# Three buffers of edge lists in a graph layer: lists and dst rows asked for three double tiles ahead

## The chip, the cores and the metric

The kernel runs on one core of one Trainium2 chip. The metric is the device time of one execution in microseconds (us). The core's engines are TensorE (PE), VectorE (DVE), ScalarE (ACT), GpSimd (POOL) and SyncE (SP, which here only asks for DMAs). A profile page and a trace of one execution go with it.

## The reference

```python
h = jnp.maximum(_layernorm(x, axis=-1), 0.0)          # x: 6250 nodes x 64
msg = h[src] + edge_attr_64                            # 206250 edges, sorted by dst
agg = jax.ops.segment_sum(msg, dst, num_segments=6250)
x = x + (jax.nn.relu(agg @ W1 + b1) @ W2 + b2)         # W1: 64x128, W2: 128x64
```

Each node sums the normalized rows of its source nodes and the features of its edges, and a small two-layer network is applied to the sum.

## The kernel before

The 6250 nodes are 49 tiles of 128. They are worked in double tiles of 256 nodes: DTS = 25 of them, numbered 0 to LAST = 24, where the last holds one tile that is cut in halves of HALF = 56.

Sum over source nodes: for a double tile the kernel makes a matrix of counts (how often does source node s feed node i) and multiplies it with h. Steps for double tile j:

- `gather_rows(j)` (POOL, indirect DMA): for each node the row of 66 sorted dst values in which its first edge lies, into g2.
- `count_below(j)` and `set_pointers(j)` (DVE): compare and reduce g2, giving the number of the node's first edge: ell_idx and rp_f.
- `place_ranges(j)` (POOL, two small instructions): first edge of each tile, r0_i. SP reads it and loads with it dst rows (`load_dst_rows`) and edge features (`load_edges`, four slots).
- `gather_slots(j)` (POOL, two indirect DMAs of 128 rows): the 64 list entries from each node's first edge on, out of comb_dram (the combined list that the kernel writes first), into ell. This is the edge list.
- `match(j)` (DVE): marks entries of other nodes, hi_m. `turn_codes(j)` (PE) transposes, `take_codes(j)` (ACT) copies to codes.
- `hots(j, b)` (DVE): one-hots lo_hot and hi_hot of five batches b (25 or 26 pairs of nodes); `count(j, u)` (PE) multiplies them, and ACT copies the counts.
- `high_sums`, `low_sums` (PE): counts times h, one double tile later, interleaved with the counts of the next.

Sum over edge features: `make_rel(j)` (POOL) turns dst rows to positions, `turn_rel(j)` (PE) transposes them, `take_rel(j)` (ACT) copies, `edge_hots(j, h)` (DVE) makes one-hots, `edge_sums` (PE) multiplies with the edges.

Every engine runs its own list of instructions in order. In DVE's loop step j the batches of `hots(j, .)` come with, in between, `edge_hots(j - 1, .)`, `match(j + 1)`, `add_rows(j - 2)`, and `count_below(j + 2)` and `set_pointers(j + 2)` behind batches 1 and 2. In PE's loop step j come the five rounds of `count(j, .)` with the sums of j - 1, the last layers of j - 2, and, in round 2, `turn_codes(j + 1)` and `turn_rel(j)`. POOL's loop is the one in the printed code below. `rest_of_h` and `rest_of_rest`, two long DVE instructions, lie behind batches 0 and 2 of double tile 0. Semaphores order the engines: a gather waits until its buffer is read (`turned`, `below_made`) and its index is made (`idx_made`); SP waits for `r0_made`, `rel_made` and `edges_done` and, at the end of its step, for `rows_added` in store_rows.

The second half-tile of the last double tile needs pointers moved by 72 partitions: PE does this with a matmul into shift_ps, and DVE copies it to ell_idx (`shifted`, `shift_made`), in loop step LAST - 2.

## Time and profile before

| what | value |
|---|---|
| median of 3 runs | 521.38 us (519.58 to 523.01) |
| the profiled execution | 519.95 us |
| its span in the trace | 518.2 us |
| mean granted clock of TensorE | 0.992 |
| PE busy | 459.3 us, 89% |
| DVE busy | 435.2 us, 84% |
| ACT busy | 380.2 us, 73% |
| POOL busy | 322.5 us, 62% |

The span is the time from the first to the last instruction that the trace shows; the execution's own time has a little more around it. Busy time counts an engine's instructions without its waits. An indirect DMA counts as busy on POOL for as long as POOL works or is held in it. PEld is PE's loading of weights, which runs beside its matmuls.

### The profile page before, as it was taken

How to read it: one execution, taken by the hardware profiler on the slowest of the kernel's cores; microseconds unless marked ns; L12 is line 12 of the kernel's file. 1: busy time of each engine (PE TensorE's matmuls, PEld its weight loads, DVE VectorE, ACT ScalarE, POOL GpSimd, SP SyncE). 2: the span in 40 equal slices, each digit the busy share in tenths (PEclk: the TensorE clock that was granted, in tenths of full speed). 3: DMA queues.
4: the chain of work that ended last, by engine and by line, in shares of the span. 5: the costliest groups of instructions: out<-in, count | busy, mean ns of one | idle time of the engine just before them, and what ended most of it. 6: DMA issues, size and time to landing. Idle time of an engine off the chain costs nothing.

```text
span 518.2 us, 27591 instructions
## 1 busy us (share of the span) xinstructions
PE 459.3 (89%) x12541; PEld 405.9 (78%) x12541; DVE 435.2 (84%) x531; ACT 380.2 (73%) x481; POOL 322.5 (62%) x223
## 2 busy tenths in 40 slices
PE   1012799999999999999999999999999999999994
PEld 1002688898889888888888988988898898888883
DVE  4989977988988998998898899889889988969550
ACT  2846766787878787787878878878787887878720
POOL 4379998976676566657756666756757675125200
PEclk9999989999999999999999999999999999999997
DMA  9758057643663474466357346536744643661200
GB/s 203 186 142 259 19 145 198 203 133 111 185 187 103 141 200 121 114 187 171 97 159 201 107 126 193 150 94 178 195 108 130 198 131 99 185 182 51 78 3 10
DMA packets 139626, 73.65 MB, mean 142 GB/s; under 512 B 23644, under 2 KB 137550, under 8 KB 139382
## 3 DMA queue, kind: packets, MB, share of 16 engines
q1 hardware_dynamic: 136105, 65.30, 45.8%
q0 software_dynamic: 3168, 4.90, 3.5%
q8 instruction: 100, 1.64, 1.2%
q10 hardware_dynamic: 234, 1.65, 1.0%
q14 instruction: 19, 0.16, 0.1%
HBM read 66.98 MB, written 4.86 MB: 139 GB/s over the span
## 4 chain that ended last, share of the span: by engine, by line
PE 84%; POOL 6%; DMA 3%; ACT 2%; DVE 2%; issue 1%; SPq 0%; ACTq 0%; DVEq 0%; POOLq 0%
PE sum_ps L844 25%; PE sum_ps L866 21%; PE count_ps L831 17%; PE sum_ps L852 14%; POOL ell L509 3%; PE sum_ps L881 3%; PE sum_ps L888 3%; POOL g L489 2%; DMA comb_rows<-counts 1%; PE sum_ps L816 1%; DMA dst_sb<-in_dst 1%; DMA ell<-comb_rows,ell_idx 1%; ACT counts L343 1%; ACT counts L345 1%; POOL r_f L496 1%
## 5 line engine op out<-in xcount | busy, mean ns | idle before, releaser
L407 ACT CAST counts<-count_ps 128x882 bf16<-128x882 f32 (+2 forms) x369 | 327.0, 978 | 60.2 <-PE count_ps L831 59.1
L675 DVE TENSOR_TENSOR lo_hot<-iota_lo,codes 128x3328 bf16<-128x3328 bf16 (+3 forms) x123 | 229.9, 1869 | 41.3 <-PE count_ps L831 25.0
L509 POOL DMA_INDIRECT ell<-comb_rows,ell_idx x50 | 105.2, 2103 | 90.2 <-DVE ell_idx L647 56.5
L844 PE MATMUL sum_ps<-counts,h_parts 128*128 128x256 bf16 (+1 forms) x1225 | 145.4, 273 | 0.0
L844 PEld LDWEIGHTS sum_ps<-counts,h_parts 128*128 128x128 bf16 x1225 | 114.5, 99 | 18.2
L831 PE MATMUL count_ps<-hi_hot,lo_hot 64*128 64x49 bf16 x6256 | 110.4, 183 | 16.8 <-DVE hi_hot L675 14.8
L831 PEld LDWEIGHTS count_ps<-hi_hot,lo_hot 64*128 64x128 bf16 x6256 | 96.0, 94 | 37.3 <-DVE hi_hot L675 19.6
L489 POOL DMA_INDIRECT g<-in_dst,row_i x49 | 95.5, 1949 | 37.9 <-DVE e_hot L689 21.3
L866 PE MATMUL sum_ps<-e_hot,edges 128*64 128x24 f32 x3528 | 112.9, 217 | 1.0 <-issue 1.0
L866 PEld LDWEIGHTS sum_ps<-e_hot,edges 128*64 128x64 f32 x3528 | 107.7, 138 | 3.7 <-issue 1.1
L675 DVE TENSOR_TENSOR hi_hot<-iota_hi,codes 128x1300 bf16<-128x1300 bf16 (+3 forms) x123 | 103.9, 844 | 0.0
L852 PE MATMUL sum_ps<-counts,h_parts 128*64 128x256 bf16 (+1 forms) x1225 | 81.1, 273 | 0.3 <-issue 0.3
L852 PEld LDWEIGHTS sum_ps<-counts,h_parts 128*64 128x64 bf16 x1225 | 62.0, 111 | 6.1 <-issue 5.7
L520 POOL TENSOR_SCALAR rel_rows<-dst_rows,tile_base 36x256 f32<-36x256 int32 (+1 forms) x25 | 47.7, 1910 | 24.3 <-DMA dst_rows<-in_dst 23.4
L689 DVE TENSOR_TENSOR e_hot<-win_tab,rel_sb 128x864 f32<-128x864 f32 x49 | 53.0, 1081 | 5.7 <-ACT rel_sb L381 5.7
L390 ACT COPY agg_sb<-sum_ps 128x256 f32<-128x256 f32 (+1 forms) x25 | 9.2, 367 | 36.3 <-PE sum_ps L852 36.3
L528 POOL TENSOR_TENSOR x_sb<-x_sb,b_all 128x128 f32<-128x128 f32 (+1 forms) x25 | 28.2, 1130 | 1.6
L805 PE MATMUL sum_ps<-ident_b,ell 128*128 128x128 bf16 x25 | 5.6, 224 | 21.7 <-DVE hi_m L661 21.7
L499 POOL CAST r_i<-r_f 1x2 int32<-1x2 f32 x24 | 22.9, 954 | 1.5
L805 PEld LDWEIGHTS sum_ps<-ident_b,ell 128*128 128x128 bf16 x25 | 2.8, 113 | 22.2 <-issue 19.3
L496 POOL TENSOR_SCALAR r_f<-rp_f 1x2 f32<-1x2 f32 x24 | 17.3, 722 | 2.5 <-DVE rp_f L649 1.9
L372 ACT COPY codes<-sum_ps 128x512 bf16<-128x512 bf16 x25 | 14.8, 593 | 5.4 <-PE sum_ps L806 5.4
(107 smaller groups left out, 213.7 us busy)
## 6 DMA issues: line engine op xcount, KB each, us to landing
edges<-in_edge_attr SPq DMA_DIRECT2D x98, 576.0 KB, 5.2
h_rows<-h_sb SPq DMA_DIRECT2D x1, 1568.0 KB, 10.3
x_sb<-in_x SPq DMA_DIRECT2D x4, 384.0 KB, 10.2
out<-o_sb SPq DMA_DIRECT2D x24, 64.0 KB, 1.7
comb_rows<-counts ACTq DMA_DIRECT2D x1, 1443.8 KB
dst_rows<-in_dst SPq DMA_DIRECT2D x49, 18.0 KB
ell<-comb_rows,ell_idx POOLq DMA_INDIRECT x50
g<-in_dst,row_i POOLq DMA_INDIRECT x49, 4.0
```

The costliest lines, as they stand in the source:

```text
L407: nc.scalar.copy(counts[j % 2][:, :, 0:2 * half].rearrange("p s (h i) -> p h s i", h=2)[:, :, :, first + a:first + b], count_ps[u % 3][:, ...
L489: nc.gpsimd.indirect_dma_start(out=g2[j % 2][:, h, :], out_offset=None, in_=dst.rearrange("(r e) -> r e", e=STEP), in_offset=bass.Indirect ...
L499: nc.gpsimd.tensor_copy(r0_i[0:1, 2 * j:2 * j + n], r0_f[0:1, 2 * j:2 * j + n]).then_inc(r0_made, 1)
L509: nc.gpsimd.indirect_dma_start(out=ell[j % 2][0:rows, h, :, :].rearrange("p s w -> p (s w)"), out_offset=None, in_=comb_dram[:, :], in_off ...
L520: nc.gpsimd.tensor_scalar(rel_rows[j % 2][0:n * CK, :], dst_rows[j % 2][0:n * CK, :], float(2 * j * P), tile_base[0:n * CK, 0:1], ALU.subt ...
L528: nc.gpsimd.tensor_tensor(x_sb[:, tiles, :], x_sb[:, tiles, :], bc(b2_all[:, :].rearrange("p (o f) -> p o f", o=1), [P, tiles_in(f), F]), ...
L675: return nc.vector.tensor_tensor(out_ap.rearrange("p i (a t) -> p i a t", t=2), bc(table_ap.rearrange("p (o a t) -> p o a t", o=1, t=2), [ ...
L689: nc.vector.tensor_tensor(e_hot[h][:, :, :].rearrange("p (c k) w -> p c k w", k=KK), bc(win_tab[:, m // LAST, :, :].rearrange("p c (o w) - ...
L831: last = nc.tensor.matmul(count_ps[u % 3][:, h, i * NT:(i + 1) * NT], lo_hot[n % 2][rows, a + i, :], hi_hot[n % 2][rows, a + i, 0:NT], sta ...
L844: nc.tensor.matmul(sum_ps[m % 2][:, 0:cols], parts[:, s, 0:2 * F], counts[m % 2][:, s, 0:cols], start=(s == 0), stop=False, skip_group_che ...
L852: last = nc.tensor.matmul(sum_ps[m % 2][half, 0:cols], parts[:, s, 2 * F:3 * F], counts[m % 2][:, s, 0:cols], start=False, stop=False, ski ...
L866: last = nc.tensor.matmul(sum_ps[m % 2][half, low:low + W], edges[t % SLOT_EDGES][:, c, k * F:(k + 1) * F], e_hot[h][:, i, :], start=False ...
```

## The change

The number of ell buffers goes from two to AHEAD = 3, with a semaphore each. POOL issues gather_rows 0 to 3, gather_slots 0 to 2, place_ranges 0 to 2 and make_rel(0) before its loop, which starts with double tile 3; in the loop make_rel and add_bias are one step further behind. DVE does `count_below(2)` before `match(0)`, `set_pointers(2)` after it, and in its loop counts and points for j + 3. The shift for the last double tile moves to loop step LAST - 3. g2, ell_idx, dst_rows, rel_rows and codes keep two buffers. The diff, without lines that only replace `j % 2` by `j % AHEAD` for ell:

```diff
+    AHEAD = 3
-        ell = [sb(f"ell{b}", [P, 2, SLOTS, 2], i32) for b in range(2)]
+        ell = [sb(f"ell{b}", [P, 2, SLOTS, 2], i32) for b in range(AHEAD)]
-        shift_ps = sum_ps[LAST % 2][:, 260:261]
+        shift_ps = sum_ps[(LAST - AHEAD) % 2][:, 260:261]
-        ell_in = [sem("ell_in0"), sem("ell_in1")]
+        ell_in = [sem(f"ell_in{b}") for b in range(AHEAD)]
...
-                    if j >= 2:
-                        pool.wait_ge(turned, j - 1)
+                    if j >= AHEAD:
+                        pool.wait_ge(turned, j - AHEAD + 1)
...
                 gather_rows(0)
-                for j in range(DTS):
-                    if j >= 3:
-                        pool.wait_ge(e_hots, 2 * (j - 3) + 1)
+                gather_rows(1)
+                place_ranges(0)
+                gather_rows(2)
+                pool.wait_ge(comb_out, 48)
+                gather_slots(0)
+                gather_slots(1)
+                place_ranges(1)
+                make_rel(0)
+                gather_rows(3)
+                gather_slots(2)
+                place_ranges(2)
+                for j in range(AHEAD, DTS):
+                    if j >= 4:
+                        pool.wait_ge(e_hots, 2 * (j - 4) + 1)
                     if j + 1 < DTS:
                         gather_rows(j + 1)
-                    if j == 0:
+                    gather_slots(j)
+                    if j < LAST:
                         place_ranges(j)
-                        pool.wait_ge(comb_out, 48)
-                    gather_slots(j)
-                    if 1 <= j < LAST:
-                        place_ranges(j)
-                    if j >= 1:
-                        make_rel(j - 1)
-                    if j >= 2:
-                        add_bias(j - 2)
+                    make_rel(j - 2)
+                    add_bias(j - 3)
+                make_rel(DTS - 2)
+                add_bias(DTS - 3)
+                make_rel(DTS - 1)
                 add_bias(DTS - 2)
                 add_bias(DTS - 1)
-                make_rel(DTS - 1)
...
                 normalize()
+                count_below(2)
                 match(0)
+                set_pointers(2)
...
-                        if b == 4 and j == LAST - 2:
+                        if b == 4 and j == LAST - AHEAD:
...
-                        if b == (1 if j + 2 < LAST else 0) and j + 2 < DTS:
-                            count_below(j + 2)
-                        if b == (2 if j + 2 < LAST else 1) and j + 2 < DTS:
-                            set_pointers(j + 2)
+                        if b == (1 if j + AHEAD < LAST else 0) and j + AHEAD < DTS:
+                            count_below(j + AHEAD)
+                        if b == (2 if j + AHEAD < LAST else 1) and j + AHEAD < DTS:
+                            set_pointers(j + AHEAD)
...
-                                if m == LAST - 2:
+                                if m == LAST - AHEAD:
                                     pe.wait_ge(shift_made, 1)
...
-                        if j == LAST - 2 and v == 3:
+                        if j == LAST - AHEAD and v == 3:
                             pe.wait_ge(rp_made, DTS)
-                            pe.wait_ge(codes_made, LAST)
-                            pe.wait_ge(rel_copied, LAST - 1)
+                            pe.wait_ge(codes_made, LAST - AHEAD + 2)
+                            pe.wait_ge(rel_copied, LAST - AHEAD + 1)
```

## Rows read from the trace of the kernel before

**Rows 1.** Stretches by double tile: length, busy us of each engine, clock, DMA.
```profile
33.80:57.06 23.26, 7.21 (x262) 6.08 (x262) 23.23 (x21) 18.06 (x18) 22.09 (x8) 1.00 0.73 215
57.06:79.35 22.29, 21.23 (x502) 17.98 (x503) 19.29 (x22) 14.94 (x19) 20.96 (x9) 0.92 0.40 113
79.35:98.77 19.42, 18.37 (x511) 16.29 (x510) 16.12 (x20) 14.63 (x19) 17.49 (x9) 1.00 0.67 169
...
118.84:137.09 18.25, 18.25 (x515) 16.23 (x509) 16.37 (x20) 14.66 (x20) 12.95 (x9) 1.00 0.52 149
```

**Rows 2.** Timeline of DVE: start, us, line, output and inputs, idle before it.
```profile
32.07 0.48 DVE L661 SCALAR_TENSOR_TENSOR hi_m<-ell,node_f 128x64 bf16<-128x64 f32 x2
33.79 1.89 DVE L675 TENSOR_TENSOR lo_hot<-iota_lo,codes 128x3328 bf16<-128x3328 bf16 x1 [1.25 <-ACT codes L372]
...
42.23 0.57 DVE L626 TENSOR_TENSOR below<-g,node_f 128x132 bf16<-128x132 int32 x1
...
45.58 3.42 DVE L641 TENSOR_TENSOR h_parts<-counts 128x3136 bf16<-128x3136 f32 x1
...
49.31 0.15 DVE L647 TENSOR_TENSOR ell_idx<-cnt,row_base 128x2 int32<-128x2 f32 x1
...
61.72 0.29 DVE L633 TENSOR_REDUCE cnt<-below 128x2 f32<-128x132 bf16 x1
...
67.38 0.48 DVE L661 SCALAR_TENSOR_TENSOR hi_m<-ell,node_f 128x64 bf16<-128x64 f32 x2 [2.82 <-DMA ell<-comb_rows,ell_idx]
```

**Rows 3.** Timeline of POOL from 27 to 66 us.
```profile
27.01 1.00 POOL L509 DMA_INDIRECT ell<-comb_rows,ell_idx  x1 [4.85 <-DMA comb_rows<-counts]
...
29.56 1.61 POOL L489 DMA_INDIRECT g<-in_dst,row_i  x1 [0.30 <-issue]
31.47 1.50 POOL L489 DMA_INDIRECT g<-in_dst,row_i  x1 [0.30 <-issue]
...
34.52 1.98 POOL L509 DMA_INDIRECT ell<-comb_rows,ell_idx  x1 [0.30 <-issue]
36.52 3.31 POOL L496 TENSOR_SCALAR r_f<-rp_f 1x2 f32<-1x2 f32 x1
...
46.13 3.70 POOL L489 DMA_INDIRECT g<-in_dst,row_i  x1 [0.30 <-issue]
50.13 12.38 POOL L509 DMA_INDIRECT ell<-comb_rows,ell_idx  x1 [0.30 <-issue]
62.81 1.81 POOL L509 DMA_INDIRECT ell<-comb_rows,ell_idx  x1 [0.30 <-issue]
...
65.20 1.15 POOL L520 TENSOR_SCALAR rel_rows<-dst_rows,tile_base 36x256 f32<-36x256 int32 x1
```

**Rows 4.** Timeline of PE: head, and one of the middle.
```profile
58.57 4.18 PE L844 MATMUL sum_ps<-counts,h_parts 128*128 128x256 bf16 x20
...
69.16 0.43 PE L816 MATMUL sum_ps<-wide,rel_rows 36*128 36x36 f32 x2
70.52 0.81 PE L831 MATMUL count_ps<-hi_hot,lo_hot 64*128 64x49 bf16 x50 [0.93 <-DVE hi_hot L675]
...
119.38 2.35 PE L844 MATMUL sum_ps<-counts,h_parts 128*128 128x256 bf16 x20
```

**Rows 5.** Stretches of one us: PE busy, granted clock, DMA share, GB/s.
```profile
72.00:73.00 1.00, 1.00 (x36) 0.79 0.37 108
...
75.00:76.00 1.00, 1.00 (x33) 0.50 0.49 99
```

**Rows 6.** All gathers of g: from the DMA to its landing, us.
```profile
DMA to landing us min/median/max: 2.3/4.0/6.9
```

**Rows 7.** Timeline of SP's queue: dst rows of double tile 1 asked.
```profile
42.45 0.82 SPq L284 DMA_DIRECT2D dst_rows<-in_dst  x2
```

**Rows 8.** Timeline of DVE: the shifted pointer of the last double tile.
```profile
462.20 0.15 DVE L774 CAST ell_idx<-sum_ps 56x1 int32<-56x1 f32 x1 [3.87 <-PE sum_ps L938]
```

**Rows 9.** Timeline of POOL in the middle: first gather of a list.
```profile
415.56 2.38 POOL L509 DMA_INDIRECT ell<-comb_rows,ell_idx  x1 [2.98 <-DVE ell_idx L647]
```

More of the change, by code:

```diff
@@ L509, in gather_slots @@
                         nc.gpsimd.indirect_dma_start(
-                            out=ell[j % 2][0:rows, h, :, :].rearrange("p s w -> p (s w)"), out_offset=None,
+                            out=ell[j % AHEAD][0:rows, h, :, :].rearrange("p s w -> p (s w)"), out_offset=None,
                             in_=comb_dram[:, :],
                             in_offset=bass.IndirectOffsetOnAxis(ap=ell_idx[j % 2][0:rows, h:h + 1], axis=0)
-                        ).then_inc(ell_in[j % 2], 16)
+                        ).then_inc(ell_in[j % AHEAD], 16)
                 def make_rel(j):
@@ L652, in match @@
                 def match(j):
-                    dve.wait_ge(ell_in[j % 2], 32 * (j // 2 + 1))
+                    dve.wait_ge(ell_in[j % AHEAD], 32 * (j // AHEAD + 1))
                     if j >= 2:
                         dve.wait_ge(turned, j - 1)
-                    words = ell[j % 2][:, :, :, :].rearrange("p h s w -> p (h s w)")
+                    words = ell[j % AHEAD][:, :, :, :].rearrange("p h s w -> p (h s w)")
                     nodes, his = words.bitcast(f32)[:, 1::2], words.bitcast(bf16)[:, 1::4]
@@ L803, in turn_codes @@
                         pe.wait_ge(rows_added, j - 2)
-                    los = ell[j % 2][:, :, :, :].rearrange("p h s w -> p (h s w)").bitcast(bf16)[:, 0::4]
+                    los = ell[j % AHEAD][:, :, :, :].rearrange("p h s w -> p (h s w)").bitcast(bf16)[:, 0::4]
                     nc.tensor.transpose(codes_ps(j)[:, 0:P], los, ident_b[:, :])
```

## The prediction, on record before the change was run

> **What bounds the kernel now.** I read the busy shares first, then the busy time by double tile, then the timelines of TensorE (PE), VectorE (DVE) and GpSimd (POOL) over the first 120 us, then what happens around the last double tiles. PE is busy 89% of the 518.2 us (the table above). By stretch: the one from 118.84 to 137.09 is a plain double tile of the middle, 18.25 us long with PE busy 18.25 us [rows 1]. Nothing that lets POOL or DVE run earlier can shorten such a stretch. Where PE is not full is the head: 7.2 of 23.3 us while double tile 0 is counted (33.80 to 57.06), 21.2 of 22.3 us in the next one, 18.4 of 19.4 us in the one after [rows 1]. The change can win or lose only there, and perhaps at the tail, where the shifted pointer is made.
>
> In the stretch of double tile 0 DVE is busy 23.2 of 23.3 us [rows 1]: it makes the one-hots and both rests of h, and PE waits for it. So whatever is added to DVE there, or makes it wait, delays the end one for one. In the stretch of double tile 1 the one wait that matters is `match(2)`: DVE idles 2.82 us until the list of double tile 2 lands [rows 2]. That list is late because of POOL: its first gather takes 12.38 us, beside DVE's one-hots, against 1.00 us for the first of list 0 [rows 3]. PE is then idle 0.93 us before the counts of batch 3 [rows 4], and from 72 to 76 us the granted clock falls to 0.79 and then 0.50, the lower of TensorE's two levels (1.2 of 2.4 GHz), and is 1.00 again after it; what PE did before was to stand idle those 0.93 us [rows 4, 5].
>
> **What can be won.** 0.93 us of idle time, and the clock. Four microseconds at 0.79, 0.50, 0.50 and 0.50 (the two outer rows are shown, the two between read 0.50) are 4 - 2.29 = 1.7 us of full-speed work lost [rows 5]. Together 2.6 us, if the match no longer waits, if the clock then holds, and if nothing else is late. The 20 matmuls that took 4.18 us at 58.57 against 2.35 us in the middle [rows 4] lost 1.8 us more at the start of PE's dense work; the change gives PE no earlier work, so I leave that term as it is. The 1.05 us that PE lacks in the stretch from 79.35 is a gap inside a run of matmuls with no wait in the code between them, so it stays.
>
> **What the change adds ahead of the one-hots.** `count_below(2)` now runs before `match(0)`. Its rows are gathered at about 22.3 us, while POOL in the kernel before stood idle 4.85 us for the combined list to be written [rows 3], so they are there. It is one compare and one reduce. In the loop the compare took 0.57 us beside a POOL instruction and the reduce 0.29 [rows 2]; without POOL each takes about 0.3, so 0.6 us. DVE has no gap before `match(0)` at 32.07 [rows 2], and everything after hangs on it: +0.6 us. (If the list of double tile 0 landed just at 32.07, a part of it would be hidden: 0 to 0.6.) `set_pointers(2)`, 0.15 us, lies in the 1.25 us that DVE waits for the codes [rows 2]: 0.
>
> **What POOL does in the new order.** After gather_slots(0) (ended 29.26 in the old order) come, in place of gather_rows(2), the gathers of list 1 with the same durations beside the same normalization, 1.61 and 1.50 us [rows 3], so to 33.0; place_ranges(1), two instructions of 0.2 us as DVE is mostly idle, to 33.4; make_rel(0), 1.15 us [rows 3], to 34.6. In the old order place_ranges(1) came beside DVE's work: its r_f alone was held from 36.52 to 39.83 [rows 3], and make_rel(0) came behind. So POOL is some 9 us earlier. Its next work is gather_rows(3), from 34.8 us, beside the one-hots. Each gather here ends 0.85 us after the end of some DVE instruction: 34.52 + 1.98 = 36.50, where lo_hot ended at 35.68; 46.13 + 3.70 = 49.83, where the second rest ended at 49.00 [rows 2, 3]. With DVE 0.6 us later the first half ends at 37.1 and the second, started behind the rest of h, 3.7 us after 37.4: 41.1.
>
> **The new wait.** DVE wants those rows early: the old `count_below(2)` at 42.23 [rows 2] found rows gathered at 29.56 to 32.97. The new `count_below(3)` stands in the same place, 42.8, and its gather ended only at 41.1. From the end of a gather to its landing it takes 2.3, 4.0 or 6.9 us (min, median, max) [rows 6]. Landing at 45.1 by the median, DVE waits 2.3 us, with 0.6 and 5.2 as the bounds. I take the median, as the edge loads of double tiles 0 and 1 are in flight: four are asked right behind match(0), and the next four come some 5 us earlier than they did, since dst rows 1 no longer wait for place_ranges(1) until 42.45 [rows 7]. Behind the waiting instruction on DVE are the one-hots of batches 2 to 4, and PE waits for those. This is in the stretch bound by DVE, so all of it counts.
>
> **The sum.** +0.6 + 2.3 - 0.9 - 1.7 = +0.3 us. While DVE waits, POOL has free room, so gather_slots(2) ends near 45 and list 2 lands before 50, against `match(2)` at 67.38 now [rows 2]: that wait is gone for certain.
>
> **The loop.** In loop step j POOL now does gather_rows(j+1), gather_slots(j), place_ranges(j), make_rel(j-2), add_bias(j-3), with its first wait one double tile earlier; DVE counts and points three ahead. The distance of each make_rel from its use on PE is unchanged, and the same number of instructions run in each double tile: 0 against a PE that is full. SP's queue, which asks for dst rows, is still held by `edges_done` (four edge slots) and by store_rows, and dst_rows has two buffers still, so past double tile 2 these come no earlier. Three list buffers give only slack. At the tail the shifted pointer moves from double tile LAST-2 to LAST-3 with the same waits; DVE idled 3.87 us for it before 462.20 [rows 8], while PE was busy all of that stretch. POOL's make_rel(22) is now queued behind it: a plain double tile earlier is 444, two gathers and it make 448, and PE turns rel 22 in the round before 462, near 458. I count 0. `count_below(5)` in the stretch from 79.35 may wait for its rows, but DVE has 3.3 us of reserve there (busy 16.1 of 19.4) [rows 1].
>
> **Rival 1, slower: make_rel(1) comes late.** On POOL make_rel(1) stands behind gather_slots(3), which must wait for set_pointers(3), at the place of the old set_pointers(2), 49.31 [rows 2]. The old order had the same queue: gather 12.38 us, until the compare before the reduce at 61.72 was over [rows 2, 3], gather 1.81, then make_rel(1) at 65.20 for PE's use at 69.16 [rows 3, 4]. But there DVE then stood still for 2.82 us, and POOL's small instructions ran free. Without that pause they meet the match and one-hots: r_f and r_i then take 0.4 to 5 us (3.31 for r_f beside the rest of h [rows 3]) and make_rel(1) up to 3, so it ends between 66.5 and 72, on DVE's own time, and PE, which wants it at 69.0, waits up to 3 us with all its counts behind, and DVE and ScalarE (codes of double tile 2 stand behind rel) after it. If the second gather is held as long as the first was, it is freed only when DVE runs dry: 64.56 and 0.6 for match and pointers and two batches of 2.5 us (67.38 + 0.6 to 70.5, when PE starts [rows 2, 4]) make 70.1, then 0.85, place_ranges and make_rel until 72.6: 3.5 us. It decides from the point where POOL is over 2.5 us later than before. Against it: in the middle the same gather after the same pointers can take 2.38 us [rows 9], not 12.38. Its time: +0.6 + 2.3 + 3 - 0.9 = +5.0, the clock loss staying: 526.4.
>
> What the rows show is that a gather beside DVE sometimes gets in at the next end of a DVE instruction (2.38 [rows 9], 1.98) and sometimes passes over ten of them (12.38) [rows 3]. The Trainium skill, SBUF — State Buffer, section "SBUF: two separate sides", says that VectorE and GpSimd share a port pair by an exclusive lock held for one whole instruction, the loser waiting until it ends; by that the gather of 12.38 us would have ended near 52 us, and make_rel(1) would always be in time, which takes Rival 1 away and leaves the forecast. The trace disagrees with its 12.38 us, so Rival 1 keeps its chance.
>
> **Rival 2, a small gain.** The rows of double tile 3 land in time: the landing takes 2.3 us, or the gather gets in at a free moment, and the 0.6 us is partly hidden. Then +0.3 + 0.3 - 2.6 = -2.0: 519.4. For it: half of the landings are under 4.0 us. Against: the edge loads.
>
> **Rival 3, nothing at all at either place.** The new wait is there but the clock dips anyway, since PE's idle time while double tile 0 is counted grows: +0.6 + 2.3 - 0.9 = +2.0: 523.4.
>
> **How the numbers follow.** The profiled execution took 519.95 us, 1.75 more than its span and 1.4 less than the median of the three runs, 521.38; I add the sum to the median: 521.7. Chances: forecast 0.35, Rival 1 0.22, Rival 2 0.23, Rival 3 0.20. All but the far end of Rival 1 is within 1% (5.2 us, about what a measurement here can tell from nothing). For the range I take Rival 2 less the spread of the runs shown (1.8): 517.6, and Rival 1 at the top: 526.5. Faster by over 1% needs 516.2 or less, over twice what the head offers: 0.02. Slower by over 1% needs a stall of PE over 3.2 us on top of the late rows: 0.10. Else 0.88.
>
> **What the changed profile would show.** Right: the middle still 18.25 us with PE full; DVE idle before the compare of `count_below(3)` near 43 us, released by the DMA of g; no idle before hi_m near 67; list gathers 0 and 1 done by 33 us; the first batch of double tile 1 on PE near 60 us instead of 57.06; the granted clock at 1.00 through 72 to 80. Wrong: if that DVE wait is missing, Rival 2; if PE idles before the transposes of rel_rows (L816 of before) near 72 us, Rival 1; a middle stretch of other than 18.2 us would upset the whole reading.

## The result, and the profile after

The changed kernel takes 526.89 us (median of 4 runs, 523.18 to 529.62) beside 521.57 of the kernel before (4 runs, 519.58 to 523.01): a ratio of 1.0103, 95% interval 1.0068 to 1.0138. It is slower by about 1%. The profiled execution took 525.78 us, with a span of 524.0 us and a mean granted clock of 0.982 (before: 519.95, 518.2 and 0.992).

The stretches by double tile of the changed kernel, cut at the same events as [rows 1] (columns: stretch and length, busy us of PE, PEld, DVE, ACT and POOL, granted clock, DMA share, GB/s):

```profile
34.40:60.28 25.88, 7.21 (x260) 6.08 (x262) 23.06 (x21) 18.09 (x18) 18.47 (x10) 1.00 0.66 197
60.28:85.11 24.83, 22.25 (x504) 19.16 (x504) 19.30 (x21) 14.86 (x19) 23.00 (x15) 0.86 0.35 100
85.11:107.33 22.22, 21.45 (x512) 18.40 (x510) 16.71 (x21) 14.65 (x19) 11.92 (x9) 0.85 0.74 191
107.33:125.58 18.25, 18.25 (x510) 16.23 (x509) 16.10 (x20) 14.72 (x19) 12.20 (x9) 1.00 0.51 148
```

The plain double tile is 18.25 us with PE full, as in [rows 1]: three buffers cost nothing in such a stretch. The three stretches ahead of it grew by 2.6, 2.5 and 2.8 us. In the first, DVE's busy time is unchanged (23.06 for 23.23) in a longer stretch, so DVE waits. In the next two the clock column fell to 0.86 and 0.85, from 0.92 and 1.00.

DVE's timeline of the changed kernel, against [rows 2]:

```profile
32.71 0.47 DVE L670 SCALAR_TENSOR_TENSOR hi_m<-ell,node_f 128x64 bf16<-128x64 f32 x2
...
45.71 0.29 DVE L635 TENSOR_TENSOR below<-g,node_f 128x132 bf16<-128x132 int32 x1 [2.75 <-DMA g<-in_dst,row_i]
...
52.55 0.15 DVE L656 TENSOR_TENSOR ell_idx<-cnt,row_base 128x2 int32<-128x2 f32 x1
...
64.63 0.28 DVE L635 TENSOR_TENSOR below<-g,node_f 128x132 bf16<-128x132 int32 x1
64.94 0.29 DVE L642 TENSOR_REDUCE cnt<-below 128x2 f32<-128x132 bf16 x1
...
67.70 0.48 DVE L670 SCALAR_TENSOR_TENSOR hi_m<-ell,node_f 128x64 bf16<-128x64 f32 x2
...
72.42 0.81 DVE L684 TENSOR_TENSOR hi_hot<-iota_hi,codes 128x1250 bf16<-128x1250 bf16 x1
```

`match(0)` starts 0.64 us later, `count_below(3)` waits 2.75 us for its rows, and `match(2)` at 67.70 waits for nothing where it waited 2.82 us. Now POOL in the same time, against [rows 3]:

```profile
34.91 2.31 POOL L490 DMA_INDIRECT g<-in_dst,row_i  x1 [0.17 <-issue]
37.53 3.71 POOL L490 DMA_INDIRECT g<-in_dst,row_i  x1 [0.30 <-issue]
41.54 1.49 POOL L510 DMA_INDIRECT ell<-comb_rows,ell_idx  x1 [0.30 <-issue]
43.33 0.95 POOL L510 DMA_INDIRECT ell<-comb_rows,ell_idx  x1 [0.30 <-issue]
...
52.96 12.78 POOL L510 DMA_INDIRECT ell<-comb_rows,ell_idx  x1 [5.78 <-DVE ell_idx L656]
66.05 1.82 POOL L510 DMA_INDIRECT ell<-comb_rows,ell_idx  x1 [0.30 <-issue]
67.89 0.20 POOL L497 TENSOR_SCALAR r_f<-rp_f 1x2 f32<-1x2 f32 x1
68.16 5.10 POOL L500 CAST r_i<-r_f 1x2 int32<-1x2 f32 x1
73.36 1.16 POOL L521 TENSOR_SCALAR rel_rows<-dst_rows,tile_base 36x256 f32<-36x256 int32 x1
```

List 2 is gathered at 41.54 and 43.33, 8.6 us ahead of the old 50.13 of [rows 3]. The lead that POOL had won stops at 52.96: `gather_slots(3)` needs pointers that DVE makes at 52.55, so POOL stood idle 5.78 us. The gather then takes 12.78 us and ends at 65.74, 0.83 us after the compare that runs until 64.91. The cast of two numbers behind it is held 5.10 us, until the last one-hot is done at 73.23 and DVE has run dry. `make_rel(1)` ends at 74.52. PE had wanted it 2.45 us earlier (against [rows 4]):

```profile
60.28 1.58 PE L842 MATMUL count_ps<-hi_hot,lo_hot 64*128 64x49 bf16 x52 [0.66 <-DVE hi_hot L684]
61.79 3.85 PE L855 MATMUL sum_ps<-counts,h_parts 128*128 128x256 bf16 x20
...
74.58 0.31 PE L827 MATMUL sum_ps<-wide,rel_rows 36*128 36x36 f32 x1 [2.45 <-POOL rel_rows L521]
...
85.87 0.70 PE L892 MATMUL sum_ps<-agg_sb,w_sb 128*128 128x256 f32 x2
...
92.05 2.04 PE L877 MATMUL sum_ps<-e_hot,edges 128*64 128x24 f32 x36 [0.77 <-issue]
```

And the stretches of one us of the changed kernel, against [rows 5] (length, PE busy, clock, DMA share, GB/s):

```profile
75.00:76.00 1.00, 1.00 (x51) 0.56 0.00 0
76.00:77.00 1.00, 1.00 (x22) 0.50 0.15 35
...
81.00:82.00 1.00, 1.00 (x48) 0.53 0.40 89
...
91.00:92.00 1.00, 0.28 (x10) 1.00 1.05 243
92.00:93.00 1.00, 0.95 (x21) 0.59 0.38 87
...
98.00:99.00 1.00, 1.00 (x7) 0.50 1.16 349
```

The rows left out of 76 to 81 and of 93 to 98 read 0.50. So the clock is at its lower level, 1.2 GHz, twice for about 7 us, and each costs 3.4 us of full-speed work, where [rows 5] lost 1.7 once. What PE did before the first fall was to stand idle 2.45 us; before the second, 0.77 us inside a run of matmuls that nothing in the code holds ("issue": no wait that the profile shows).

To follow the loss along PE, take its mark at the first layer of double tile 0: 80.12 us before, 85.87 now, 5.75 later. Of this 3.2 is already there when the counts of double tile 1 start (57.06 to 60.28), 1.5 is the wait for rel (2.45) less the 0.93 of [rows 4], and 1.7 the deeper clock dip. That is 6.4; the -0.7 left I can't split (a part is that the first 20 sums took 3.85 for 4.18). One double tile on (100.61 and 108.09) the marks are 7.5 us apart: the second gap and dip cost the changed kernel about 4.2, and the kernel before has gaps of 1.05 and 0.88 us there. By the last mark 5.9 are left (the spans differ by 5.8). The kernel before loses 0.7 us near 265, in a gap of the same "issue" kind, and 0.9 between its marks at 448.11 and 485.34, two double tiles of 18.61 and 18.62 us where the changed kernel takes 18.25 and 18.06; no run here says why. So only the part up to the first dip has a chain of waits that leads back to the change. The second dip follows a gap that no wait explains.

### The profile page after: what moved, and what is told of

It is laid out like the page before. It is cut to its first block, busy times and chain, and to the rows that moved or that the text cites. A ratio compares the mean times of both kernels' runs of the same rounds, so it can differ in the third digit from the quotient of the medians.

```text
span 524.0 us, 27589 instructions
## 1 busy us (share of the span) xinstructions
PE 462.5 (88%) x12541; PEld 408.9 (78%) x12541; DVE 434.1 (83%) x531; ACT 380.2 (73%) x481; POOL 307.3 (59%) x223
## 4 chain that ended last, share of the span: by engine, by line
PE 84%; POOL 5%; DMA 4%; issue 2%; DVE 2%; ACT 2%; SPq 0%; ACTq 0%; POOLq 0%
PE sum_ps L855 25%; PE sum_ps L877 21%; PE count_ps L842 17%; PE sum_ps L863 13%; POOL ell L510 4%; PE sum_ps L892 3%; PE sum_ps L899 3%; DMA g<-in_dst,row_i 2%; DMA comb_rows<-counts 1%; PE sum_ps L827 1%; DMA dst_sb<-in_dst 1%; ACT counts L344 1%; ACT counts L346 1%; DVE counts L609 1%; POOL rel_rows L521 0%
## 5 line engine op out<-in xcount | busy, mean ns | idle before, releaser
L510 POOL DMA_INDIRECT ell<-comb_rows,ell_idx x50 | 92.8, 1855 | 94.9 <-DVE ell_idx L656 63.7
L855 PEld LDWEIGHTS sum_ps<-counts,h_parts 128*128 128x128 bf16 x1225 | 115.2, 99 | 18.8
L842 PEld LDWEIGHTS count_ps<-hi_hot,lo_hot 64*128 64x128 bf16 x6256 | 96.6, 95 | 37.4 <-DVE hi_hot L684 18.8
L490 POOL DMA_INDIRECT g<-in_dst,row_i x49 | 87.7, 1790 | 50.3 <-DVE e_hot L698 34.7
L877 PE MATMUL sum_ps<-e_hot,edges 128*64 128x24 f32 x3528 | 114.7, 219 | 0.8 <-issue 0.8
L877 PEld LDWEIGHTS sum_ps<-e_hot,edges 128*64 128x64 f32 x3528 | 109.5, 140 | 3.5 <-issue 0.8
L684 DVE TENSOR_TENSOR hi_hot<-iota_hi,codes 128x1300 bf16<-128x1300 bf16 (+3 forms) x123 | 105.3, 856 | 0.0
L521 POOL TENSOR_SCALAR rel_rows<-dst_rows,tile_base 36x256 f32<-36x256 int32 (+1 forms) x25 | 44.3, 1771 | 27.9 <-DMA dst_rows<-in_dst 27.5
L529 POOL TENSOR_TENSOR x_sb<-x_sb,b_all 128x128 f32<-128x128 f32 (+1 forms) x25 | 35.8, 1434 | 1.7
L500 POOL CAST r_i<-r_f 1x2 int32<-1x2 f32 x24 | 32.3, 1344 | 1.5
L382 ACT COPY rel_sb<-sum_ps 128x72 f32<-128x72 f32 (+1 forms) x25 | 5.7, 227 | 18.4 <-PE sum_ps L827 18.4
```

Of the source, the lines that this page charges most:

```text
L490: nc.gpsimd.indirect_dma_start(out=g2[j % 2][:, h, :], out_offset=None, in_=dst.rearrange("(r e) -> r e", e=STEP), in_offset=bass.Indirect ...
L500: nc.gpsimd.tensor_copy(r0_i[0:1, 2 * j:2 * j + n], r0_f[0:1, 2 * j:2 * j + n]).then_inc(r0_made, 1)
L510: nc.gpsimd.indirect_dma_start(out=ell[j % AHEAD][0:rows, h, :, :].rearrange("p s w -> p (s w)"), out_offset=None, in_=comb_dram[:, :], in ...
L521: nc.gpsimd.tensor_scalar(rel_rows[j % 2][0:n * CK, :], dst_rows[j % 2][0:n * CK, :], float(2 * j * P), tile_base[0:n * CK, 0:1], ALU.subt ...
L529: nc.gpsimd.tensor_tensor(x_sb[:, tiles, :], x_sb[:, tiles, :], bc(b2_all[:, :].rearrange("p (o f) -> p o f", o=1), [P, tiles_in(f), F]), ...
L684: return nc.vector.tensor_tensor(out_ap.rearrange("p i (a t) -> p i a t", t=2), bc(table_ap.rearrange("p (o a t) -> p o a t", o=1, t=2), [ ...
```

## The experiments

Several theories were set against each other after the result. A: the loss is the two new waits of the head, DVE's for the rows of double tile 3 and PE's for `make_rel(1)`, and the clock behind them. B: the third buffer itself costs time in the loop, and the head is only shifted. C: with one wait taken out the other grows by as much. D: the clock dips whatever the waits do. The kernels with whole edge loads ran on three chips. On the first the kernel before itself took 528.03 to 543.10 us, so ratios there are broad, and I repeated three of the kernels elsewhere; the repeats carry the verdicts.

**One wait each, and both.** Edits to the changed kernel:

```diff
# rel_ahead: on POOL
                 place_ranges(2)
+                make_rel(1)
...
-                    make_rel(j - 2)
+                    if j >= 4:
+                        make_rel(j - 2)
# rows_later: on DVE, count_below and set_pointers one batch later for double tile 0
-                        if b == (1 if j + AHEAD < LAST else 0) and j + AHEAD < DTS:
+                        if b == (2 if j == 0 else 1 if j + AHEAD < LAST else 0) and j + AHEAD < DTS:
# all three: both, and
-                count_below(2)
                 match(0)
+                count_below(2)
```

> The changed kernel with make_rel(1) ahead of POOL's loop, behind place_ranges(2), so that it stands no longer behind gather_slots(3). Theory A (the loss is the sum of 0.6 us of DVE work ahead of match(0), 2.75 us of DVE waiting for the rows of double tile 3, and 2.45 us of PE waiting for make_rel(1), with the clock that falls after it): no idle of PE ahead of the transposes of rel_rows near 72 us, the first dip of the clock shorter or gone, a time 2.5 to 5 us under the changed kernel's, 522 to 524.5, ratio to before 1.000 to 1.006. The DVE wait of 2.75 us stays. Rival B (POOL's loop or the middle is slower for three buffers, the head is only shifted): the ratio stays at 1.010.

> The changed kernel with count_below(3) and set_pointers(3) one batch later on DVE (behind batches 2 and 3 of double tile 0). Theory A: no DVE wait of 2.75 us, the counts of double tile 1 start on PE near 57.6 us in place of 60.28; the wait for make_rel(1) stays, as gather_slots(3) still stands ahead of it: 2.5 to 3 us under the changed kernel's time, ratio to before 1.003 to 1.007. Rival C (the later pointers keep POOL longer, so that the wait of PE for make_rel(1) grows by what DVE gained): ratio stays at 1.008 to 1.012, with the PE wait over 4 us. Rival B: 1.010 with both waits changed as under A.

> The changed kernel with both edits and count_below(2) behind match(0), where DVE waits for the codes. Theory A: all three losses gone, match(2) waits for nothing: 1 to 2.6 us under the kernel before, 519 to 520.6, ratio 0.994 to 0.999. Rival B: over 1.005 even so. If the clock's dips are independent of the waits (Rival D): the waits are gone but granted clock of 0.5 still shows between 65 and 100 us for several us, ratio 0.998 to 1.004.

On the first chip the ratios were 1.0207 [1.0122, 1.0293], 1.0187 [1.0034, 1.034] and 1.0126 [1.0005, 1.0247]: too broad to rank. The traces were not. `make_rel(1)` ahead removed PE's wait alone (DVE still waited 3.02 us); rows later removed DVE's wait, and PE's as well, which I had not expected; all three removed both. Elsewhere, beside the changed kernel again:

> The changed kernel itself once more, beside the experiments of this call. If the head is as in its first trace: DVE waits 2.8 us ahead of count_below(3), PE 2.5 us ahead of the transposes of rel_rows, the counts of double tile 1 start on PE near 60.3 us, the last layers of double tile 0 near 86 us (80.12 in the kernel before); ratio 1.007 to 1.014. If the place of these waits is chance: they move by over 1 us or are missing.

> The kernel with the three edits once more. Theory A: no DVE wait for g, no PE wait for rel_rows, last layers of double tile 0 on PE near 77.5 us plus what PE waits for nothing that the trace shows; ratio to before 0.994 to 1.000. Rival B (three buffers cost in the loop): 1.005 or more with that head.

> make_rel(1) ahead of the loop, once more. Theory A: no PE wait for rel_rows, the DVE wait for g of 2.8 us stays, ratio to before 1.002 to 1.007, 1.5 to 5 us under the changed kernel of this call. If the clock falls without that wait too (as it did on the chip before, where PE had gaps of its own): 0 to 2.5 us under it.

> count_below(3) and set_pointers(3) one batch later, once more. As in its first trace: no DVE wait for g, gathers of list 3 in 2.3 us each, make_rel(1) done near 62 us and so no PE wait for it, counts of double tile 1 on PE near 57.3 us. With gaps in PE's matmuls as in the kernel with the three edits: ratio 0.998 to 1.003.

| kernel | median us | ratio to before, 95% | DVE waits for rows | PE waits for rel |
|---|---|---|---|---|
| changed | 526.31 | 1.0095 [1.0070, 1.0119] | 2.88 | 2.05 |
| make_rel(1) ahead | 526.99 | 1.0095 [1.0058, 1.0132] | 2.82 | none |
| rows later | 522.02 | 1.0021 [0.9987, 1.0055] | none | none |
| all three | 519.76 | 0.998 [0.995, 1.001] | none | none |

The kernel before took 521.07 us on that chip (24 runs), and 521.32 on the one of the row "rows later" (35 runs). With both waits out, all else of the change in place, the time is that of the kernel before: freed of the two waits the change costs no more than 0.1% (the upper end of the interval), and a plain double tile takes 18.25 us with two buffers and with three, so B falls. C falls with the rows later, where the other wait went too. What the change costs comes with the waits. D is half right: the kernel with all three edits has no wait in the head, and the clock still reads 0.50 there for about 3 us, behind a gap. Moving the counting by one batch does nearly all of it. Its POOL timeline shows why rel is in time too:

```profile
52.63 2.29 POOL L510 DMA_INDIRECT ell<-comb_rows,ell_idx  x1 [0.30 <-DVE ell_idx L656]
55.23 2.22 POOL L510 DMA_INDIRECT ell<-comb_rows,ell_idx  x1 [0.31 <-issue]
...
60.28 1.64 POOL L521 TENSOR_SCALAR rel_rows<-dst_rows,tile_base 36x256 f32<-36x256 int32 x1
...
66.20 12.77 POOL L510 DMA_INDIRECT ell<-comb_rows,ell_idx  x1 [0.66 <-DVE ell_idx L656]
```

The same gather that was held 12.78 us at 52.96 takes 2.29 at 52.63. The hold of 12.77 us is still there, but one list later, and no engine waits for what is behind it.

That `make_rel(1)` ahead won nothing, where A had forecast a ratio of 1.002 to 1.007, though PE's 2.05 us were gone, has another reason: gaps of 1.48 and 1.61 us came in at 82.45 and 89.73, and the clock was at its lower level for about 7 us behind the second. They are taken up below.

**What the repeat of the changed kernel adds.** Its waits are those of the first trace (2.88 and 2.05 us, counts of double tile 1 from 60.36), and so is the first dip of the clock, from 76 to 83 us. The second dip is missing. At the mark of double tile 1 it is 3.7 us behind the trace of the kernel before (104.26 against 100.61), and 3.2 at 469.90 against 466.72. Then PE stops once more:

```profile
484.69 1.06 PE L877 MATMUL sum_ps<-e_hot,edges 128*64 128x24 f32 x30 [2.11 <-issue]
```

The double tile around it takes 22.20 us, and the last mark is 6.8 us behind. Of the ten traces off the first chip with whole loads, those shown here and below, five have such a gap (0.94 to 2.11 us, at 482 to 487) and take 20.7 to 23.5 us for that double tile, where the others take 18.1 to 18.6: four of the eight with three buffers, and one of the two with two. No wait leads to it, and whether the change makes it likelier is not shown. So of the 6.8 us between these two traces 3 to 4 stand in the head and the rest in a late gap, where in the first pair 7.5 stood in the head. The medians, 5.3 us apart, are over executions with and without such gaps.

**What holds POOL.** I put a DVE instruction with one small input between the one-hots, which does no work for the result:

```diff
# in the kernel before
                         hots(j, b)
+                        if b == 3 and j == 0:
+                            nc.vector.tensor_reduce(gap[:, :], iota_w[:, :], AX.X, ALU.add)
# in the changed kernel: behind batches 3 and 4
+                        if b >= 3 and j == 0:
+                            nc.vector.tensor_reduce(gap[:, b - 3:b - 2], iota_w[:, :], AX.X, ALU.add)
```

> The kernel before with one tiny reduce (128x24 to 128x1, its result unused) on DVE between batches 3 and 4 of double tile 0, while POOL is in the gather that took 12.38 us. If a one-input reduce lets POOL in (as the ends of the long gathers, 0.85 us after the start of the reduce of count_below, suggest): the gather takes 4 to 5 us in place of 12.4, the DVE wait of 2.82 us before match(2) and PE's 0.93 us go, ratio 0.994 to 0.999. If the gather is held for another reason (the idle time of DVE, its ring of descriptors): 12 us stay, ratio 1.000.

> The changed kernel with two tiny one-input reduces on DVE, behind batches 3 and 4 of double tile 0. If such a reduce lets POOL in: the gathers of list 3 take 2 to 3 us each in place of 12.8 and 1.8, make_rel(1) ends near 61 us in place of 74.5, PE's wait ahead of the transposes of rel_rows is gone, the DVE wait for g stays; ratio 1.002 to 1.007. If the 12.8 us has another cause, it stays, and so does the ratio of 1.010.

The first gather, 12.38 us in [rows 3], of the kernel before with the reduce (which DVE ran from 52.10 to 52.27):

```profile
50.32 2.68 POOL L510 DMA_INDIRECT ell<-comb_rows,ell_idx  x1 [0.30 <-issue]
53.30 9.47 POOL L510 DMA_INDIRECT ell<-comb_rows,ell_idx  x1 [0.30 <-issue]
```

It ended at 53.00, and the next one, started 0.30 us later and so a us after the reduce, was held until 62.77, past eight one-hot instructions, to the next reduce (61.99). DVE's reduce:

```profile
52.10 0.17 DVE L766 TENSOR_REDUCE gap<-iota_w 128x1 f32<-128x24 f32 x1
```

In the changed kernel with two reduces, POOL and then DVE:

```profile
52.91 3.08 POOL L511 DMA_INDIRECT ell<-comb_rows,ell_idx  x1 [5.80 <-DVE ell_idx L657]
56.30 2.23 POOL L511 DMA_INDIRECT ell<-comb_rows,ell_idx  x1 [0.30 <-issue]
58.55 6.55 POOL L498 TENSOR_SCALAR r_f<-rp_f 1x2 f32<-1x2 f32 x1
...
65.44 2.74 POOL L522 TENSOR_SCALAR rel_rows<-dst_rows,tile_base 36x256 f32<-36x256 int32 x1
```

```profile
55.08 0.17 DVE L777 TENSOR_REDUCE gap<-iota_w 128x1 f32<-128x24 f32 x1
...
57.62 0.17 DVE L777 TENSOR_REDUCE gap<-iota_w 128x1 f32<-128x24 f32 x1
```

Both gathers were let in at a reduce (55.08 and 57.62), and the next small instruction was held 6.55 us to the next one, 65.06. So the hold is DVE's doing, and one instruction of 0.17 us ends it; the edit changed nothing else. That rel came at 68.2, not 61 as I expected, is this last hold. PE's wait was gone, and the time 523.66 us, 1.0041 [1.0015, 1.0067], between changed and before (the trace is of its slowest execution, 528.17). The other reading, that the DMAs in flight hold the gather, falls, as the edit asks for no other ones ahead of it.

The other traces agree. In all twenty, 23 gathers took over 4.5 us, and each ended 0.82 or 0.83 us after the end of a DVE instruction. Behind that instruction came a reduce in 16 cases; in the other seven DVE stood still, for 0.09 us in the shortest. In none did another two-input instruction follow at once. (Shorter gathers get in beside ordinary one-hots too, as the 2.29 us above.) Nor is it enough that an instruction is short: the compare of 0.28 us (64.63 in the changed kernel) has two inputs, and the gather was held to its end and not to its start. No run has a longer one-input instruction there, or one of another kind. In the kernel before the reduce won nothing (539.26 beside 537.29 on the first chip, too broad for a verdict), though the wait of `match(2)`, PE's 0.93 us and the dip were all gone: gaps of 0.81, 1.26 and 0.79 us in PE's matmul runs had come in their place.

**Where the rest goes: gaps without a wait.** PE's timeline of the kernel with all three edits has these rows with idle time:

```profile
78.34 0.33 PE L844 MATMUL count_ps<-hi_hot,lo_hot 64*128 64x49 bf16 x12 [1.48 <-issue]
...
85.89 1.18 PE L879 MATMUL sum_ps<-e_hot,edges 128*64 128x24 f32 x35 [1.88 <-issue]
```

And of its stretches of one us, PE alone (length, PE busy, clock, DMA share, GB/s):

```profile
77.00:78.00 1.00, 0.00 (x0) 1.00 1.27 285
...
88.00:89.00 1.00, 1.00 (x26) 0.50 0.29 52
```

PE runs a list of equal matmuls with nothing to wait for, and stops; behind the second gap the clock is at its lower level for 3 us (1.7 us lost). The gaps stand where the DMA engines are busiest, some of it the store of h_rows (1568 KB), which SP asks for in step 2. I moved that store to step 8:

```diff
-                    if j == 2:
+                    if j == 8:
                         with nc.allow_non_contiguous_dma(reason="the first dst of each following row"):
```

> The kernel with the three edits, and the store of h_rows and the loads of each row's next dst asked in SP's step 8 in place of step 2. Seen so far: with the waits of DVE and PE gone, PE has gaps inside its runs of matmuls near 78 and 85 us (1.48 and 1.88 us) while that store (1568 KB) and the loads are in flight, and the clock falls behind the second. Theory E (PE's instructions come late while the DMA engines are full, and this eats what the edits win): without the store there the gaps near 78 and 85 us shrink to under 0.5 us each and the dip of the clock there is gone, ratio to before 0.990 to 0.996; a gap may show later, where the store now is. Rival F (the gaps belong to the program's place, not to the traffic): they stay at 1.4 and 1.9 us, ratio 0.996 to 1.000.

> The kernel before with the same store in step 8. Theory E: its one gap of 1.05 us near 85.5 is gone or halved; the head's other waits stay: ratio 0.996 to 1.000. Rival F: gap stays, 1.000.

> make_rel(1) ahead of the loop, with the store in step 8. It won nothing over the changed kernel when the store was in step 2 (1.0095 both): PE's wait for rel_rows of 2.05 us was gone, gaps of 1.48, 1.61 and 0.49 us came in. Theory E: those gaps are gone or under 0.5 us each, ratio 1.001 to 1.006. Rival F: 1.008 to 1.011.

| kernel, store moved | median us | ratio to before, 95% | gaps over 0.45 us (start of the work behind them) |
|---|---|---|---|
| all three | 519.22 | 0.9973 [0.9945, 1.0002] | 1.48 (78.41), 0.85 (194.35) |
| before | 522.57 | 1.0029 [1.0003, 1.0056] | 1.43 (74.97), 1.12, 0.87, 1.33 (196 to 214), 0.94 (483.63) |
| make_rel(1) ahead | 524.18 | 1.0051 [1.0019, 1.0083] | 0.56, 1.27 (100.81), 1.83 (207.56) |

The gap near 86 goes with the store, in all three (it was the 1.61 us at 89.73 with `make_rel(1)` ahead), and new ones come up near 194 to 214; SP asks for the store at 186.94 in the kernel with all three edits. The one near 78 stays at 1.48 us there, shrinks to 0.56 with `make_rel(1)` ahead, and one of 1.43 us comes into the kernel before, which had none. So neither E nor F is right as a whole. The first ratio is F's, the third E's, and the second lies above both. No gain is shown: the kernel before became 0.3% slower, and the intervals of the other two overlap those with the store in step 2.

So I counted. The ten traces taken off the first chip with whole loads (before, changed twice, and the seven others) have 30 such gaps over 0.45 us behind 60 us (five are of the slowest execution named above). In 26 of them the DMA engines were at least 0.8 busy in the 3 us ahead; of all stretches of 3 us in the kernel before that is so in 50 of 146. The last test takes that traffic away. Every edge load past the first four slots brings 64 KB in place of 576; the rest of a slot keeps an older tile's features, so the edge sums are not the reference's, but each instruction and wait is there:

```diff
+                    n = CK // 2 if t < SLOT_EDGES else 1
...
-                        sp.dma_start(edges[t % SLOT_EDGES][:, c:c + CK // 2, :],
-                                     edge[bass.ds(first + c * CHUNK, RANGE // 2), :].rearrange(
+                        sp.dma_start(edges[t % SLOT_EDGES][:, c:c + n, :],
+                                     edge[bass.ds(first + c * CHUNK, n * CHUNK), :].rearrange(
```

> The three edits (make_rel(1) ahead, the counting one batch later, match(0) before count_below(2)), and every edge load past the first four slots brings one chunk of 64 KB in place of 576 KB; the rest of the slot keeps the features of an earlier tile, so the edge sums are not the reference's; every instruction and wait is there. Theory A (the gaps in TensorE's matmul runs come of full DMA engines, behind which its instructions arrive late): the 1.48 us gap near 78 and the 1.88 near 85 are gone or under 0.5, gaps over 0.45 us sum to under 1 us where they were 4.3, no clock at half after 66 us, and the time is 514 to 517 us. Theory B (they come of the order of the instructions alone): the same gaps at the same places, 519 to 520 us.

> The kernel before with the same cut of the edge loads; the edge sums are not the reference's. Theory A: the gaps of 1.05 (86.57) and 0.88 us (100.33) are gone, the wait for the list of double tile 2 and the clock dip behind it stay: 519 to 520 us, about 2 us under before. Theory B: gaps and time as before, 521.

> The changed kernel with the same cut of the edge loads; the edge sums are not the reference's. Both theories: gather_slots(3) is still held some 12.8 us and TensorE still waits some 2 us for rel_rows of double tile 1, with the clock at half behind it. DVE's wait for the rows of double tile 3 stays at 2.8 us, since the first four edge loads are whole. Theory A: 3 to 4 us above the three edits with cut loads by the two waits, and the second clock dip gone; Theory B: 6 to 7 us above them, as with whole loads.

> The three edits with the edge loads past the first four slots cut to one chunk of 64 KB, again; the edge sums are not the reference's. On the first chip the gaps in TensorE's matmul runs were 0.90 us at 83.70 and three of 0.5 near 87, and none past 90. Theory A (gaps come of full DMA engines): no gap over 0.45 us past 100 us and less than 2.5 us of them in all; 515 to 518 us where the whole loads gave 519.76. Theory B (order alone): 519 to 520.

> The kernel before with cut edge loads, again; the edge sums are not the reference's. Theory A: no gap over 0.45 us past 100 us, 519 to 520 us. Theory B: 521. The wait for the list of double tile 2, 0.9 us of TensorE, may be shorter, as the gathers meet fewer DMAs.

> The changed kernel with cut edge loads, again; the edge sums are not the reference's. Both theories: the 2 us wait for rel_rows of double tile 1 and the clock at half behind it stay. Theory A: 6 to 9 us above the three edits with cut loads, the whole price of DVE's 2.8 us, TensorE's 2 us and 3.4 us of clock, and no gap past 100 us; Theory B: 6 to 7 us above, with whole loads as with cut ones, and gaps past 100 us.

In both sets the kernel before with whole loads took 526.8 to 545.7 us beside them. The first was on the chip of the repeats, where the same kernel had taken 521.07, so this isn't a matter of the chip alone. The second set:

| kernel, cut edge loads | median us (range) | ratio to before with whole loads |
|---|---|---|
| all three edits | 523.61 (520.99 to 524.33) | 0.9797 [0.9724, 0.9870] |
| before | 525.41 (523.92 to 525.92) | 0.9830 [0.9762, 0.9899] |
| changed | 532.76 (531.13 to 536.31) | 0.9987 [0.9946, 1.0029] |

The first set read 525.36, 527.77 and 536.98, the last from 527.04 to 540.78, which settles nothing. In all six traces no gap over 0.45 us stands past 97 us, the late one at 482 to 487 included; with whole loads, `make_rel(1)` ahead had eight of them on the first chip, and ten traces of the other chips had 16. The 1.48 near 78 is gone; what is left in the head with all three edits is 0.60 and 0.51 us (0.90, 0.46, 0.56 and 0.48 in the first set). The times that theory A gave, 514 to 518 us for the three edits and 519 to 520 for the kernel before, were all missed, by 5 us and more: a plain double tile takes 18.5 to 18.9 us in these traces and 18.25 in [rows 1]. The kernel before with the reduce shows 18.8 as well, on the first chip with whole loads, so this is not the cut; its cause is open. Theory A of these runs holds for the late gaps as far as this: they come with the edge loads. That they are full DMA engines holding up PE's instructions fits, but no row shows it.

The table also has the price of the change without the late gaps. The changed kernel is 9.2 us over the three edits (theory A said 6 to 9, B 6 to 7) and 7.4 over before, but the second number is too small for a price. The trace of the kernel before with cut loads has a wait that it hasn't with whole ones:

```profile
88.17 1.09 PE L832 MATMUL count_ps<-hi_hot,lo_hot 64*128 64x49 bf16 x52 [2.35 <-DVE hi_hot L676]
```

A gather of rows was held there 11.88 us from 68.24, DVE waited 5.65 us for the rows and PE 2.35 us for DVE, and the clock fell behind it (0.62 and 0.53 in the stretches of 2 us from 88 to 92). It is the same kind of chain in another place: a held gather, then DVE and PE waiting.

Two stretches of the three edits with cut loads (length, PE busy, clock, DMA share, GB/s):

```profile
34.00:60.00 26.00, 10.09 (x317) 1.00 0.68 202
60.00:84.00 24.00, 23.43 (x587) 1.00 0.35 82
```

The same two of the changed kernel with cut loads:

```profile
34.00:60.00 26.00, 7.20 (x260) 1.00 0.66 196
60.00:84.00 24.00, 18.68 (x405) 0.80 0.08 22
```

PE works 2.9 us less up to 60, and 4.8 less from there to 84; the clock at 0.80 is 4.8 us of full speed in 24. The last two overlap, as much of PE's idle time falls while the clock is low and is then in both, so their sum, 12.5, is over the 9.2 measured. Half of the 4.8 us that PE lacks is the wait for rel, 2.41 us; most of the rest is small gaps behind it, up to 0.95 us.

## Why the prediction was wrong

The forecast of 521.7 us failed, and the time of 526.89 lies 0.4 us above the range; Rival 1, priced at 526.4, came.

- **Added ahead of the one-hots, +0.6.** Right: 0.64, and `set_pointers(2)` was free.
- **The new wait, +2.3.** Right in place and mechanism, 2.75 us, within its bounds (2.88 in the repeat). The first counts of double tile 1 came at 60.28, as forecast.
- **The match of double tile 2.** Right: its wait is gone, lists 0 and 1 being gathered by 33.1 us and list 2 by 44.3 (forecast near 45).
- **The loop and the tail, 0.** Right: 18.25 us, and the three edits have them at no cost that shows. In the first pair of traces the changed kernel even gains 0.9 us near the end.
- **The step that failed: the sum's -0.9 and -1.7.** I gave back PE's 0.93 us and the clock's 1.7 as if nothing else were late at that place, with the argument that POOL has free room while DVE waits. It had, but `gather_slots(3)` can't use it: its pointers are made behind that very wait, at 52.55, 3.2 us later than the old 49.31. The lead of 9 us was lost in 5.78 us of idle time, and PE's wait for rel (2.45, 2.05 in the repeat) took the place of the one for the match. The clock, which was to stay at 1.00 from 72 to 80 us, was at 0.50 for about 7 us and lost 3.4 us in place of the 1.7 that I gave back.
- **Rival 1.** Its chain was right: the gather passes over ten DVE instructions, the small ones behind it meet a DVE that no longer pauses, the release comes when DVE runs dry. One link was another: I had the second gather held until then, at 70.1 us; it took 1.82 us, and the cast behind it was held, until 73.23, as the late rows had moved DVE too. The stall, priced at 3, was 2.45. The clock loss, which I let stay at 1.7, doubled to 3.4. That 526.4 came so near is in part luck: the terms on the trace (+0.64, +2.75, +2.45 - 0.93, +1.7 for the clock) make 6.6, a second gap and dip came on top (4.2), and the kernel before lost 1.9 us in two gaps there and more later, which took some of it off again. In the repeat the sum is made up otherwise, with the late gap. Its chance of 0.22 was too low: every link had a row of its own in the trace of before, and the one thing in the way was a single gather of 2.38 us from the middle [rows 9].
- **Rival 2, Rival 3.** Neither came. Rival 3's reason, the clock dips anyway, was a part of what did.
- **The port lock.** The held gathers and the two reduces bear on it. The Trainium skill, SBUF — State Buffer, section "SBUF: two separate sides", has a DVE instruction hold the port pair for that one instruction. The trace disagrees on the length of the hold: POOL was passed over at the end of ten of them (12.78 us) and let in at a short reduce, so the measurement decides against it for this kernel. That the hold is this lock at all, no run shows.

Still open is why the gather at 52.63 in the kernel with the rows later got in at the end of an ordinary one-hot (54.10, its own end 0.82 us behind), when the one at 52.96 did not. DVE's row:

```profile
52.29 1.81 DVE L684 TENSOR_TENSOR lo_hot<-iota_lo,codes 128x3200 bf16<-128x3200 bf16 x1
```

The gather did so on both chips. And what stays of the gaps near 80 us with cut loads has no cause that I can show.

The three edits at 519.76 us, and 519.22 with the store moved, are the best versions found; both intervals reach 1, so a gain over the kernel before is not shown. Over the changed kernel it is 6.5 us.

## What to carry to other kernels

A lead in time is only as long as the next thing that it needs: for each instruction that is moved ahead, find the first one on its engine whose input is still made at the old time, and see who queues behind it. When an engine's pause is removed, look for whom that pause served. Where an engine is full, as PE is here, a stall can cost its length and then the clock behind it: the wait of 2.45 us was followed by 3.4 us lost at the lower clock. And when a difference of 1% is read from two traces, compare their marks along the engine that is full: here one trace had all of the loss in the head, and the other about half of it near 485 us, in a gap that no wait connects with the change.

## What the runs showed that I had not expected

- POOL's gather and even its instructions on two numbers (r_f, and the cast r_i) were held 12.78, 6.55 and 5.10 us beside two-input instructions of DVE; a one-input reduce (0.17 us the added ones, 0.29 the kernel's own) ended the hold of a gather or of r_f at each of the five places where one was met (52.10 and 61.99 with one reduce added, 55.08, 57.62 and 65.06 with two). All 23 gathers of over 4.5 us in the twenty traces ended at such a reduce or at a pause of DVE.
- The granted clock fell to 0.50 behind an idle time of 2.45 us as of 0.77 us, and stayed there for about 7 us; after 1.48 us near 78 with all three edits it did not fall. Idle time alone doesn't tell.
- Matmul runs with nothing to wait for have gaps of 0.5 to 2.1 us. Cutting edge loads to a ninth removed those past 97 us, and on a chip on which the kernel before took 535.04 us it made that kernel 1.7% faster (0.9830 [0.9762, 0.9899]), though no wait in the trace of before names an edge load. What a removed wait wins can be lost again in such gaps: `make_rel(1)` ahead freed PE's 2.05 us and had gaps of 5.2 us in all where the changed kernel had 2.1, at the same time of 526 to 527 us.
